# An attention block followed by a top-2 mixture of eight experts on one core: padding rows written during attention, expert weights loaded and split earlier, and nothing of the expert weights between the last batch's routing steps

## The reference, cut to what matters

```
x = x + attention(layernorm(x), ctx)          # 32 batches, 112 rows of 256; ctx 375 rows of 192; 16 heads of 64
x = x + experts(layernorm(x))                  # 3584 rows

# attention:  q = x @ Wq; k, v = ctx @ Wkv; softmax(q k^T / 8) v; @ Wproj + bproj
# experts (E = 8, FF = 512, top 2):
probs = softmax(x @ gate_w); p, idx = top_k(probs, 2); p = p / sum(p)
gate, up = split(x @ gate_up_w[e]); h = silu(gate) * up; y_e = h @ down_w[e]
out = sum over the two chosen experts of p * y_e
```

## Time and profile before

| | PE | PEld | DVE | ACT | POOL |
|---|---|---|---|---|---|
| busy us of the span of 1619.5 | 1540.4 | 1356.4 | 916.2 | 812.7 | 551.2 |
| share | 95% | 84% | 57% | 50% | 34% |

### The profile page before, as it was taken

One profiled execution on the slowest core, in us unless ns is written; L12 is line 12 of the kernel. 1 busy time (PEld: TensorE's weight loads), 2 busy tenths in 40 slices (PEclk: granted clock), 3 DMA queues, 4 the chain that ended last, 5 costly groups with the idle time before them and its releaser, 6 DMA issues. The chain is left out here.

```text
span 1619.5 us, 37428 instructions
## 1 busy us (share of the span) xinstructions
PE 1540.4 (95%) x12134; PEld 1356.4 (84%) x12135; DVE 916.2 (57%) x2482; ACT 812.7 (50%) x2186; POOL 551.2 (34%) x607
## 2 busy tenths in 40 slices
PE   5999999999999999999999999999995499999997
PEld 4888988888988988898889898888984388888886
DVE  4566666666666665666666566666656433333332
ACT  4655555555655655565565555555555122222221
POOL 4224233433323332433333332333246232233332
PEclk9999999999999999999999999999998699999999
DMA  5100001000001100000100000111014433333332
GB/s 156 40 25 22 28 24 29 21 27 21 27 21 34 32 21 27 24 27 21 32 21 27 21 27 21 28 36 65 12 34 178 135 51 52 52 52 49 50 51 30
DMA packets 53104, 66.60 MB, mean 41 GB/s; under 512 B 6624, under 2 KB 48336, under 8 KB 52816
## 3 DMA queue, kind: packets, MB, share of 16 engines
q1 hardware_dynamic: 36560, 42.65, 9.2%
q0 software_dynamic: 12336, 16.19, 6.1%
q10 hardware_dynamic: 4176, 7.34, 1.3%
HBM read 44.85 MB, written 21.31 MB: 41 GB/s over the span
## 5 line engine op out<-in xcount | busy, mean ns | idle before, releaser
L698 ACT ACTIVATE prob<-bank,neg_max 112x375 f32<-112x375 f32 x512 | 294.9, 579 | 349.0 <-DVE neg_max L933 349.0
L933 DVE TENSOR_REDUCE neg_max<-bank 112x1 f32<-112x375 f32 x512 | 244.8, 541 | 78.9 <-PE bank L1146 76.1
L1156 PE MATMUL bank<-ident,prob 112*125 112x112 f32 x1536 | 212.3, 272 | 2.2 <-ACT prob L698 2.2
L1156 PEld LDWEIGHTS bank<-ident,prob 112*125 112x125 f32 x1536 | 198.4, 188 | 15.1 <-ACT prob L698 4.6
L818 DVE TENSOR_TENSOR K_l<-bank,K_h 128x376 fp32r<-128x376 f32 x256 | 140.7, 550 | 106.1 <-ACT K_h L669 105.3
L648 POOL DMA_INDIRECT out<-y_out,dest_now x63 | 97.9, 1554 | 247.6 <-ACT y_out L786 219.1
L1068 PE MATMUL bank<-Wgu,hT_h 128*128 x504 | 176.4, 432 | 1.1 <-DVE hT_l L1027 1.1
L1175 PE MATMUL bank<-probT,V 125*64 125x112 f32 x3072 | 175.5, 263 | 0.0
L565 POOL CAST OT_h<-O_now 128x448 fp32r<-128x448 f32 x64 | 35.7, 557 | 382.4 <-DVE O_now L863 382.4
L1175 PEld LDWEIGHTS bank<-probT,V 125*64 125x64 f32 x3072 | 148.0, 137 | 18.3 <-issue 0.4
L667 ACT COPY V<-bank 125x512 f32<-125x512 f32 x192 | 112.4, 586 | 88.8 <-PE bank L1119 84.3
(11 more groups left out here) (162 smaller groups left out, 3671.7 us busy)
## 6 DMA issues: line engine op xcount, KB each, us to landing
h_in<-bins SPq DMA_DIRECT2D x63, 129.0 KB, 2.1
y_sb<-in_ctx SPq DMA_DIRECT2D x32, 187.5 KB, 2.4
y_sb<-in_ctx SPq DMA_DIRECT2D x64, 93.8 KB, 2.5
Wgu<-in_L_ffn_gate_up_w SPq DMA_DIRECT2D x4, 1024.0 KB, 5.4
Wgu<-in_L_ffn_gate_up_w ACTq DMA_DIRECT2D x4, 1024.0 KB, 8.0
x_sb<-in_x SPq DMA_DIRECT2D x16, 224.0 KB, 2.6
x_res<-in_x SPq DMA_DIRECT2D x32, 112.0 KB, 2.3
out<-x SPq DMA_DIRECT2D x32, 112.0 KB, 1.9
```

Of the source, the lines that this page charges most:

```text
L698: nc.scalar.activation(prob[:, j, :], S_ps[j][0:LQ, 0:LKV], ACT.Exp, bias=neg_max[:, j:j + 1], accum_out=row_sum[:, head // HB, head % HB: ...
L933: nc.vector.tensor_reduce(neg_max[:, j:j + 1], S_ps[j][0:LQ, 0:LKV], AX.X, ALU.max, negate=True).then_inc(max_done, 1)
L1156: last = nc.tensor.transpose(S_ps[j][0:KR, t * LQ:t * LQ + LQ], prob[:, j, t * KR:t * KR + KR], ident[0:LQ, 0:LQ])
```

## The change

- **Weights at the start.** The four tiles of `Wkv` become eight of half the width, for K (`WkH`, `WkT`, `WkL`, `WkU`) and V (`WvH` and so on). There are four casts and four subtractions of 128x1024 instead of two and two of 128x2048, all before the cast of `Wq`. `Wq` is loaded after the third low part, `Wproj` after the fourth.
- **Padding.** During attention SyncE writes padding over the whole of `bins`, one block of 8 x 128 rows of 1032 bytes (1.06 MB) per batch, 29 blocks; a batch's scatter waits until the blocks that it can reach are filled. The eight padding writes behind the bins, and `pad_row`, go.
- **Buffers.** The context buffers, `xn` and `xT` lie where `Wd` of experts 2 to 7 goes, and no longer where `Wgu` goes. `Wd` of experts 0 and 1 is loaded in the 15th pair, the other six are loaded by SyncE in the last batch.
- **Expert weights.** Experts 1 and 2 are loaded in batch 31 before the store of batch 30, expert 3 after the last V product. 4 and 5 go on ScalarE's queue after the last scores, then 6 and 7. GpSimd splits 0, 1, 2: 1 after `x_bias` of batch 31, 2 after the scatter of batch 29. ScalarE casts 3 and 4 before the last `gates`, 5 after them, 6 and 7 after tile 0's cast; VectorE takes the low part of 3 before the last residual, of 4 and 5 after `plan`, of 6 and 7 after tile 0's low part. TensorE waits for experts 0 and 1 as tile 0 and 1 need them, and for all eight before tile 2.

```diff
@@ buffers
+        WkH, WkL, WkT, WkU = (sb(f"Wk{n}", [P, HD], F32R) for n in "HLTU")
+        WvH, WvL, WvT, WvU = (sb(f"Wv{n}", [P, HD], F32R) for n in "HLTU")
-        early = -(-(part1_end - wd_at) // (FJ * C * 4))
+        early = 2
+        place["at"] = wd_at + early * FJ * C * 4
+        y_sb = sb("y_sb", [P, 2, 2, LKV], F32)
...
@@ SyncE
+            def prefill(k, slot):
+                rows = blocks[k:k + 1] if known(k) else blocks[bass.ds(k, 1)]
+                sp.dma_start(rows.rearrange("o p e w -> (o p) e w"),
+                             pad_rows[:].unsqueeze(1).to_broadcast([P, E, W])).then_inc(prefilled[slot], 16)
-            sp.wait_ge(w_lo, 1)
+            sp.wait_ge(w_lo, 3)
             sp.dma_start(raw[:, 0, :], Wq.rearrange("(k p) n -> p k n", p=P)).then_inc(raw_in[0], 16)
-            sp.wait_ge(w_lo, 2)
+            sp.wait_ge(w_lo, 4)
             sp.dma_start(raw[:, 1, :], Wproj.rearrange("(k p) n -> p k n", p=P)).then_inc(raw_in[1], 16)
...
+                    if known(i) and i == NP - 1 and odd:
+                        sp.wait_ge(made, a.made(a.find(0, "q", 7)))
+                        load_expert(sp, 1)
+                        sp.wait_ge(made, a.made(a.find(0, "K", HP - 1)))
+                        load_expert(sp, 2)
...
                     if known(i) and i == NP - 1 and odd:
-                        sp.wait_ge(made, a.made(a.find(0, "q", 7)))
-                        load_expert(sp, 1)
                         sp.wait_ge(made, a.n0 + len(a.items))
-                        for e in (2, 3):
-                            load_expert(sp, e)
+                        load_expert(sp, 3)
+                        sp.dma_start(Wd[:, early:E] ...).then_inc(wd_in, 16)
+                    if there(b + 2, STRIDE // P):
+                        sp.wait_ge(prefilled[odd], 16 * (i + 1))
+                        prefill(b + 2, odd)
...
-            for e, start in zip(range(E // 2, E), pad_starts):
-                sp.dma_start(bins[bass.ds(start, P), :], pad_rows[:, e, :]).then_inc(pads_late, 16)
@@ GpSimd
+                    if known(i) and i == NP - 1 and odd:
+                        split_expert(1)
                     if there(b - 1, B):
                         pool.wait_ge(ag2, b)
...
+                    if known(i) and i == NP - 1 and odd:
+                        split_expert(2)
                     if there(b, B):
                         split_O(2 * b, 0, b)
...
-            for e in range(E // 2):
-                pool.indirect_dma_start(bins, ... pad_rows[:, e, :], None).then_inc(pads_out, 16)
@@ ScalarE
-            hi_of_weight(WkvH[:], 0, 1)
-            hi_of_weight(WkvT[:], 1, 2)
+            hi_of_weight(WkH[:], 0, k_cols, 1)
+            hi_of_weight(WkT[:], 1, k_cols, 2)
+            hi_of_weight(WvH[:], 0, v_cols, 1)
+            hi_of_weight(WvT[:], 1, v_cols, 2)
...
+                        if known(i) and i == NP - 1 and odd and s == NS - 1:
+                            act.wait_ge(scores_made, B * H)
+                            for e in (4, 5):
+                                load_expert(act, e)
...
-            act.dma_start(Wd[:, 0:early] ...).then_inc(wd_in, 16)
+            hi_of_experts(6, E)
@@ VectorE
+                        if known(i) and i == NP and not odd and s == 0:
+                            lo_of_expert(3)
...
-            lo_of_experts(6, E)
+            for e in (4, 5):
+                lo_of_expert(e)
...
             lo_of_rows(0, 0)
             keep_dest(0, 0, 0)
+            for e in (6, 7):
+                lo_of_expert(e)
```

More of the change, by code:

```diff
@@ L535, in _, with scatter @@
             pool.tensor_tensor(wp_lo, raw[:, 1, :], wp_hi.bitcast(F32), ALU.subtract).then_inc(wp_done, 1)
-            def scatter(b, slot):
+            def scatter(b, slot, blocks_before):
                 pool.wait_ge(row_done, b + 1)
@@ L540, in scatter @@
                 pool.wait_ge(kept, 2 * b + 2)
+                even, odd = ((b + 2) // 2, (b + 1) // 2) if known(b) else blocks_before
+                pool.wait_ge(prefilled[0], 16 * (min(even, 15) if known(b) else even))
+                if not known(b) or b >= 1:
+                    pool.wait_ge(prefilled[1], 16 * (min(odd, 14) if known(b) else odd))
                 pool.sem_inc(passed, 1)
@@ L611, in pair @@
                     if there(b - 2, B):
-                        scatter(b - 2, odd)
-                    if known(i) and i == NP and not odd:
-                        pool.wait_ge(wgu_hi, 4)
-                        lo_of_expert(5)
+                        scatter(b - 2, odd, (i, i - 1 + odd))
+                    if known(i) and i == NP - 1 and odd:
+                        split_expert(2)
                     if there(b, B):
@@ L623, in pair @@
                         split_expert(0)
-                    if known(i) and i == NP - 1 and odd:
-                        split_expert(1)
             over_pairs(pool, pair, 2)
-            pool.wait_ge(plan, 1)
-            for e in range(E // 2):
-                pool.indirect_dma_start(bins, bass.IndirectOffsetOnAxis(ap=pad_row[:, e:e + 1], axis=0),
-                                        pad_rows[:, e, :], None).then_inc(pads_out, 16)
             for slot in range(2):
@@ L878, in residual, with lo_of_expert @@
                 nc.vector.bn_aggr(mv2[:], stat2[:]).then_inc(ag2, 1)
-            def lo_of_experts(first, end):
-                for e in range(first, end):
-                    dve.wait_ge(wgu_hi, e - 1)
-                    nc.vector.tensor_tensor(Wgu[:, e, 1], Wgu[:, e, 1].bitcast(F32), Wgu[:, e, 0].bitcast(F32),
-                                            ALU.subtract).then_inc(wgu_lo[1], 1)
+            def lo_of_expert(e):
+                dve.wait_ge(wgu_hi, e - 2)
+                dve.wait_ge(wgu_ready, e)
+                nc.vector.tensor_tensor(Wgu[:, e, 1], Wgu[:, e, 1].bitcast(F32), Wgu[:, e, 0].bitcast(F32),
+                                        ALU.subtract).then_inc(wgu_ready, 1)
             def choose(b):
@@ L1095, in make @@
                     c = slice(arg * P, arg * P + P)
-                    last = product_ctx(dst[:, 0:LKE], c, slot, slice(0, LKE), True)
+                    last = product_ctx(dst[:, 0:LKE], (WkH, WkL, WkT, WkU), c, slot, slice(0, LKE), True)
                 elif kind == "q":
@@ L1108, in make, with product_ctx @@
                         slot = odd
-                    c = slice(HD + half * 512, HD + half * 512 + 512)
-                    last = product_ctx(dst[0:KR, :], c, slot, slice(t * KR, t * KR + KR), False)
+                    if a.first:
+                        pe.wait_ge(w_lo, 4)
+                    c = slice(half * 512, half * 512 + 512)
+                    last = product_ctx(dst[0:KR, :], (WvH, WvL, WvT, WvU), c, slot, slice(t * KR, t * KR + KR), False)
                 last.then_inc(made, 1)
-            def product_ctx(dst, c, slot, rows, weights_stay):
-                todo = [(WkvH[:, c], yA_h[:, slot, rows]), (WkvH[:, c], yA_l[:, slot, rows]),
-                        (WkvL[:, c], yA_h[:, slot, rows]), (WkvT[:, c], yB[:, slot, rows]),
-                        (WkvU[:, c], yB[:, slot, rows])]
+            def product_ctx(dst, weights, c, slot, rows, weights_stay):
+                high, low, tail, tail_low = (w[:, c] for w in weights)
+                todo = [(high, yA_h[:, slot, rows]), (high, yA_l[:, slot, rows]), (low, yA_h[:, slot, rows]),
+                        (tail, yB[:, slot, rows]), (tail_low, yB[:, slot, rows])]
                 for n, (w, y) in enumerate(todo):
@@ L1296, in gate @@
                 pe.wait_ge(hT_lo, t + 1)
+                if known(t) and t < 2:
+                    pe.wait_ge(wgu_ready, e + 1)
+                elif known(t) and t == 2:
+                    pe.wait_ge(wgu_ready, E)
                 if not known(t) or t >= 2:
```

101 lines of the change are left out of this document (43 added, 58 removed).

## The result

| | before | changed |
|---|---|---|
| median us | 1621.44 (1621.09 to 1624.04, 4 runs) | 1607.84 (1607.10 to 1609.05, 4 runs) |
| profiled execution us | 1621.27 | 1607.10 |
| its span | 1619.5 | 1605.3 |

The ratio is 0.9913, with a 95% interval of 0.9896 to 0.9931: faster by 13.6 us. The forecast was 1607 us with a range of 1601 to 1613.5.

The account below looks back on a forecast made before the run. TensorE bounds attention, the routing, padding and first-load chain the end. -17.5 (seam) - 5.0 (`Wd`) + 0.1 + 0.6 + 6.0 (start) + 1.5 (lock) = -14.3 us from 1621.27: forecast 1607 us, own range 1603 to 1611, 8-in-10 range 1601 to 1613.5.

Parts of the forecast that it names:

- the start: First weight loads: `Wq` asked for 4.8 us later, plus 1.2 us of slower TensorE pace; 6.0 us added to the end.
- the padding: Seam after batch 31: without the eight padding writes SyncE goes on at the scatter's landing, 6.8 us sooner.
- the loop: Attention batches: padding blocks cost 0, bounds 0 to 2 us; rival that they hold the loop up, 1639 us, chance 0.05.
- the seam: Routing of batch 31 to tile 0's first load: `hn`, a `Wgu` low part and padding go, 17.5 us less.
- the tiles: First expert tiles: no wait for `Wd`, and 5.17 us per tile as before.
- `hn`: Seam: 4.96 us link, itself about 1.2 us, the rest blocked by VectorE's low parts; 3.75 us go.
- the 7.02 us link: Seam, between `top_i` and `mark`: the `Wgu` low part goes whole, 7.0 us less.
- `Wd` stall, low parts of 6 and 7: First tiles: 5.0 us gained as TensorE no longer waits for `Wd`, 0.6 lost to low parts before tile 1's.
- low part of 3 before the residual: Batch 31, VectorE: expert 3's low part ahead of the residual costs about 0.1 us.
- split of expert 1 in batch 31 (the lock): GpSimd's split blocks VectorE through shared ports, maxima 1.5 us late; bounds 0 and 2.5.
- the row named: Batch 31, VectorE: `dest` of batch 29 would be held by GpSimd's subtraction and take some 4.5 us.
- The collision of the weights: Rival: `Wd` and experts 3 to 7 load together, expert 4 lands late, `gates` waits 5 us: 1612 us, chance 0.17.

Follow-up runs that it names:

- experiment 7: Kernel before, with VectorE's low part of expert 4 moved from the first largest-two step of batch 31 to behind `plan`: 1620.28 us, ratio 0.9982.
- experiment 10: Kernel before, with VectorE's low part of expert 4 moved behind `plan` and GpSimd's of expert 5 behind the padding writes: 1616.39 us, ratio 0.9957.
- experiment 5: Kernel before, with padding blocks written during attention and without the eight padding writes at the seam: 1616.02 us, ratio 0.9958.
- experiment 4: Changed kernel with the old padding: eight writes behind the bins, no blocks during attention: 1618.25 us, ratio 0.9975 to the kernel before.
- experiment 6: Changed kernel with `Wd` of experts 2 to 7 loaded by ScalarE behind tile 0's cast, as before: 1611.94 us, ratio 0.9924 to the kernel before.
- experiment 1: Changed kernel with half casts and low parts reordered, `Wq` asked for after the second low part: 1603.92 us, ratio 0.9887 to the kernel before.
- experiment 2: Changed kernel with GpSimd's split of expert 1 waiting until VectorE ended `mark` of batch 29: 1606.98 us, ratio 0.9903 to the kernel before.
- experiment 3: Changed kernel with `Wq` asked for early and `mark` of batch 29 ahead of expert 1's split: 1600.58 us, ratio 0.9872 to the kernel before.
- experiment 8: The kernel before run once more, unchanged, as a control for differences between two profiles: 1620.82 us.
- 12: Changed kernel with early `Wq`, `mark` before expert 1's split, and 20 extra TensorE products before batch 31's projection: 1601.29 us, ratio 0.9863 to the kernel before.

## Why the prediction was right, step by step

The number came out within 1 us of the forecast, and that is closer than the terms deserve: the start cost 1.8 us less than forecast and the padding gave 0.5 more, the loop and the clock cost 1.3 and 1.55 that I had not forecast, and these nearly cancel. What was right is the seam and the tiles.

The step from `x` of batch 31 to the load of tile 0's rows was measured in seven kernels:

| kernel | us | gone against before |
|---|---|---|
| before | 33.18 | |
| 7, VectorE's low part moved | 31.11 | 2.1 |
| 10, GpSimd's moved too | 26.33 | 6.9 |
| 5, padding alone | 25.87 | 7.3 |
| 4, changed but for the padding | 22.70 | 10.5 |
| 6, changed but for `Wd` | 15.37 | 17.8 |
| changed | 15.38 | 17.8 |

| term | forecast | profiles | how it is shown |
|---|---|---|---|
| `hn` | -3.75 | -3.7 | a link of 4.96 before, 1.25 for one now; argued, no run of its own |
| the 7.02 us link | -7.0 | -6.8 | experiment 10 |
| padding | -6.8 | -7.3 | experiments 4 and 5 |
| `Wd` stall, low parts of 6 and 7 | -5.0 + 0.6 | -4.05 | experiment 6: 4 to 6 for the stall |
| low part of 3 before the residual | +0.1 | 0 | hidden behind the wait for the projection |
| start | +6.0 | +4.2 | experiment 1 |
| split of expert 1 in batch 31 (the lock) | +1.5 | +1.2 | experiments 2 and 3: 0.6 to 0.75 goes with the order, 0.56 stays |
| attention loop | 0 | +1.3 | not explained |
| clock in the projection | 0 | +1.55 | varies between executions, experiment 8 |
| sum | -14.3 | -13.6 | |

The ledger is that of the shift in the tiles. The two profiled executions differ by 14.2 us; the other 0.6 lie behind the last tile's products.

- **The seam** was right, 17.55 us in its three terms (17.5 in the sum) against 17.80 measured in the whole. `hn` 3.7, link 6.8 and padding 7.3 add up to that. The nice agreement has one hole: I said that the low part "goes whole", as if it were one thing. Experiment 7 shows that it was two, and that the sum is right only because the change also takes GpSimd's split away from there.
- **The padding** was worth 7.3 where I had 6.8, for the scatter lands sooner than the 3.7 us that I gave it, and `plan`, 5.3 us behind `bin_row`, is the last to release the load. That VectorE's low parts of 4 and 5 would end with nothing to spare was right too: tile 0's low part began 0.60 us behind its cast's start, where it was 0.39 before.
- **The start** is the term with the largest error, and it depends on the execution. Five profiles of kernels with the old start begin 1.84 us before to 0.43 us after the first (mean -0.5). Six with the changed start begin at +3.83 to +5.84 (mean +4.5). So the edit costs 5.0 us. I had taken 4.8 for the load, which holds (4.7 with the sooner landing taken out), and 1.2 for TensorE's pace after the wait, which was 0.5.
- **The lock.** The step over batch 31 was 1.2 us, near the forecast 1.5, but only about half of it went when `mark` was put ahead of the split (experiment 3), and the row named was the wrong one: `dest` took its usual 0.15 us, and `top_f` and `chosen` were blocked in its place. My own numbers said so: `chosen` of before started at 1206.52 (and `top_f` at 1206.11), within the cast that I had placed at 1205.8 to 1207.7. By the rule of the Trainium skill (SBUF — State Buffer, section "SBUF: two separate sides") the other engine waits for a whole instruction of the one that holds the shared ports. The trace agrees, with 1.50 us under the cast and 4.44 under the subtraction, and it shows a one-input cast of 112x2 blocked as well as an operation with two SBUF inputs. Other operations went through: VectorE's `probT` copy out of a bank at 1210.79 to 1211.71 was not held up by the cast that began at 1211.20, nor were `x` and its statistics by the subtraction in experiment 2.
- **The collision of the weights** (chance 0.17) did not come. `Wd` landed at 1243.65 and expert 4 at 1245.24, 7.52 us after its issue where it took 5.02 without `Wd` (experiment 6): the two loads overlapped and it cost 2.5 us. Its cast ended at 1247.17, 5.4 us before `gates`.
- **The attention loop** is longer by 1.3 us. This I had put at 0, a change of the loop's length was one of my signs of being wrong, and I do not explain it. It belongs to the kernel: 0.9 to 1.4 us in seven profiles with the changed buffers and padding blocks, 3.7 and 3.8 in two without the blocks, -0.2 to +0.5 in four profiles of the old kernel and its variants, with blocks (experiment 5) or without. TensorE's idle time is the same (busy 398.14 us of 400 in 400 to 800 us in both), so its instructions take longer, by 0.04 us per batch. In experiment 4 most of the 3.8 us lies in the products that make V. One of the kinds that grew most, before and there (60 to 1180 us: busy us, mean ns):

```profile
L1119 PE MATMUL bank<-WkvT,yB 128*125 128x512 f32 x178 | 70.0, 393 | 0.0
```

```profile
L1126 PE MATMUL bank<-WvT,yB 128*125 128x512 f32 x178 | 71.4, 401 | 0.0
```

  In the changed kernel it is 395 ns. The blocks' traffic is not the cause; what in the new code or layout is, no run tells apart.
- **The clock** in the projection cost 1.3 to 2.4 us in eleven of fourteen profiles of all kernels. The first profile of before was one of the three without it (the others are experiments 3 and 12), so 1.55 us of the ledger are the luck of that profile. In the profiles of experiments 2, 4 and 6 it also fell once inside batch 31, and cost 1.3 to 1.5 us more.

## What to carry to other kernels

When a long link of a chain is an instruction of VectorE that ran beside a large one of GpSimd, its length is not its price. Ask what is left if only this one goes: here the next VectorE instruction, a cast of 112x2, took over the wait until GpSimd was done, and both had to move. It depends on the instruction: `x` (one input from a bank), its statistics and the row maxima ran beside the same subtraction at their usual times. And where an edit is about the end of a program, read its first 20 us too: a load that waits for a later low part cost 5 us at the start, about a quarter of what the rest won (21.9 us), and a new order of the four half casts and low parts gave it back.

## What the hardware showed that I had not expected

- Casting 224 numbers took VectorE 0.16 us with GpSimd idle, 1.50 when it began 0.42 us into a cast of 128x2048, and 4.86 beside a subtraction of 128x2048 (experiment 7); both times it ended with GpSimd's operation. Beside the same subtraction the statistics of 112x256 kept their 0.43 us (experiment 2).
- The granted clock of TensorE fell to 0.50 around a projection that began 2.8 us after the last product, in eleven profiles of fourteen, with the same 24 products (0.28 us each at 1.00, 0.41 at 0.50); two profiles of the kernel before differ in it. At 0.50 it is the 1.2 GHz level.
- Landings of the first loads vary: the same cast of `Wkv`'s second half began at 15.41 and at 13.52 us in two executions of the kernel before, and the whole program moved with it.
- 30 MB of writes beside attention (29 blocks, median 6.1 us each from issue to landing) raised the landing of the next `x_res` from 2.3 to 5.5 us and cost the loop nothing (experiment 5).
